# Products of ones in TensorE's order: the feed-forward stages and the router steps of a two-layer kernel

## The reference, cut to what matters

```
x = x + 0.5 * L0_ffn(layernorm(x))      # ffn1
x = x + L0_attn(layernorm(x))
x = x + 0.5 * L0_ffn(layernorm(x))      # ffn2
x = x + 0.5 * L1_ffn(layernorm(x))      # moe1
x = x + L1_attn(layernorm(x))           # retention
x = x + 0.5 * L1_ffn(layernorm(x))      # moe2

def L0_ffn(x):                          # 8 experts of rank 8
    result = x @ base_w.T + base_b
    gating = softmax(x @ router_w.T + router_b)          # then bfloat16
    mid = x @ lora_A
    return result + 2.0 * einsum('bsr,erd,bse->bsd', mid, lora_B, gating)

def L1_ffn(x):                          # 16 experts, 4 of them per token
    scores = sigmoid(x @ router_w.T)
    ... the two best of 4 groups, the four best experts in them, weights tw ...
    routed = sum over the chosen experts of tw * (silu(x @ gate_w) * (x @ up_w)) @ down_w
    return routed + (silu(x @ sh_gate_w) * (x @ sh_up_w)) @ sh_down_w
```

## Time and profile before

| what | us |
|---|---|
| median of 3 runs | 1731.96 |
| lowest and highest of them | 1723.12, 1746.84 |
| the profiled execution, its own time | 1735.6 |
| its span in the trace | 1733.8 |

### The profile page before, as it was taken

The page is one execution under the profiler, slowest core; times in us unless marked ns, Lnnn a source line. Parts: engine busy times, 40 slices in busy tenths (PEclk is TensorE's granted clock), DMA queues, the critical chain, the costliest instruction groups (busy, mean ns, idle before and its releaser), DMA issues. The chain is left out here.

```text
span 1733.8 us, 36975 instructions
## 1 busy us (share of the span) xinstructions
PE 1537.2 (89%) x10054; PEld 1258.9 (73%) x10054; DVE 1167.2 (67%) x4550; ACT 815.3 (47%) x1995; POOL 796.3 (46%) x1129
## 2 busy tenths in 40 slices
PE   6699999999897757999959999999999686699995
PEld 5477777777587546888847888887888574588884
DVE  6448888888575743555548898988898666255554
ACT  2247777777625213444424555555555431244442
POOL 2246666666524240222217786877787504111111
PEclk9759999999956778999979999999999868899998
DMA  4598000000023010001021111111111001000003
GB/s 126 149 300 225 0 0 0 0 0 0 7 80 116 18 37 14 27 26 27 27 72 42 41 38 38 37 37 37 37 37 38 1 2 37 25 26 27 25 27 110
DMA packets 101116, 82.91 MB, mean 48 GB/s; under 512 B 9820, under 2 KB 88351, under 8 KB 100720
## 3 DMA queue, kind: packets, MB, share of 16 engines
q1 hardware_dynamic: 95178, 69.87, 15.1%
q0 software_dynamic: 4416, 9.58, 1.6%
q10 hardware_dynamic: 1382, 1.83, 0.4%
HBM read 23.71 MB, written 40.75 MB: 37 GB/s over the span
## 5 line engine op out<-in xcount | busy, mean ns | idle before, releaser
L892 DVE SCALAR_TENSOR_TENSOR moe_block_act<-banks,moe_taken,moe_block_gated 128x128 f32<-128x128 f32 x592 | 166.8, 344 | 186.4 <-ACT moe_block_gated L936 179.1
L921 POOL DMA_INDIRECT y_rows<-moe_block_y,moe_taken x74 | 71.4, 965 | 383.2 <-ACT moe_block_y L946 383.2
L1181 DVE CUSTOM_DVE_ANT_0 attn_z<-banks,rel_bias 128x128 f32<-128x128 f32 (+1 forms) x512 | 161.9, 353 | 69.9 <-PE banks L1311 63.1
L1229 POOL TENSOR_TENSOR attn_z<-attn_top,attn_z 128x256 f32<-128x256 f32 x256 | 159.3, 630 | 94.2 <-DVE attn_top L1181 93.4
L1706 ACT ACTIVATE ret_normed<-banks,ret_head_shift,ret_head_rstd 128x128 f32<-128x128 f32 x256 | 103.9, 458 | 157.0 <-DVE ret_head_shift L1620 157.0
L936 ACT ACTIVATE moe_block_gated<-banks 128x512 f32<-128x512 f32 x148 | 88.6, 599 | 159.2 <-PE banks L977 159.0
L993 PE MATMUL banks<-moe_down,moe_block_actT 128*128 x1184 | 156.3, 275 | 0.0
L1258 ACT ACTIVATE attn_prob<-banks 128x384 f32<-128x384 f32 x256 | 125.9, 492 | 50.2 <-PE banks L1318 40.2
L1318 PE MATMUL banks<-ident,attn_z 128*128 128x128 f32 x768 | 144.0, 299 | 0.3 <-ACT attn_z L1253 0.3
L993 PEld LDWEIGHTS banks<-moe_down,moe_block_actT 128*128 128x128 f32 x1184 | 143.8, 192 | 0.3
L975 PE MATMUL banks<-moe_hi,moe_block_x_hi 128*128 x296 | 130.8, 442 | 1.6 <-DVE moe_block_x_lo L882 1.5
(11 more groups left out here) (260 smaller groups left out, 4255.4 us busy)
## 6 DMA issues: line engine op xcount, KB each, us to landing
slots<-moe_pad SPq DMA_DIRECT2D x12, 2304.0 KB, 20.0
ret_twins<-ret_twins SPq DMA_DIRECT2D x256, 64.0 KB, 2.0
moe_taken<-slots SPq DMA_DIRECT2D x74, 72.0 KB, 1.8
moe_back<-y_rows SPq DMA_DIRECT2D x16, 256.0 KB, 5.0
moe_stage<-in_moe_w SPq DMA_DIRECT2D x4, 576.0 KB, 7.1
bias_reversed<-scratch SPq DMA_DIRECT2D x1, 2048.0 KB, 9.6
out<-x_res SPq DMA_DIRECT2D x8, 256.0 KB, 4.5
ret_stage<-in_ret_w SPq DMA_DIRECT2D x16, 96.0 KB, 2.2
```

The lines of the kernel that those rows point to most:

```text
L892: last = dve.scalar_tensor_tensor(act_f[:, i, at], ps_u[:, i, at], taken[:, b % RB, column:column + 1], gated[:, i, at], ALU.mult, ALU.mult)
L1181: last = dve.tensor_tensor_reduce(out=z[:, k % Z, cols], in0=ps_s[:, k % 2, cols], in1=bias, scale=1.0, scalar=-3.0e38, op0=ALU.add, op1=A ...
L1229: pool.tensor_tensor(z[:, k % Z, P:WIDTH], top[:, k % Z, 1:2].to_broadcast([P, WIDTH - P]), z[:, k % Z, P:WIDTH], ALU.subtract).then_inc(s ...
```

## The change

A tile `ones` (128 x 512, bfloat16) is filled by GpSimd in the opening block. A helper issues a number of products of it with itself, each 128 x 512, into PSUM. Nobody reads the result, and the helper neither waits nor signals. It is called with 3 products at three places: ahead of the wait of `transpose_x` and of `transpose_om` in both feed-forward stages (into a bank of its own, the eighth), and ahead of the wait of `router` in both routing parts (into `ps_y`, which the shared expert uses only later). This makes 16 calls in each feed-forward stage and 8 in each routing part, 48 calls and 144 products. Nothing is removed.

```diff
+def keep_busy(pe, bank_out, ones, times):
+
+    for _ in range(times):
+        pe.matmul(bank_out, ones[:, 0:P], ones[:, :], start=True, stop=True)
...
         ps_y = bank([P, 2, GT])
+        ps_spare = bank([P, 512])
...
             def transpose_x(it, u):
+                keep_busy(pe, ps_spare, ones, 3)
                 pe.wait_ge(xn_ready, count(it, u))
...
             def transpose_om(it, u):
+                keep_busy(pe, ps_spare, ones, 3)
                 pe.wait_ge(om_ready, count(it, u))
...
             def router(g):
                 s = g * GROUP // SEG
+                keep_busy(pe, ps_y[:, :], ones, 3)
                 pe.wait_ge(x_split, g + 1)
...
+        ones = sb("ones", [P, 512], BF16)
...
                     pool.memset(neg_half[:, :], -0.5)
+                    pool.memset(ones[:, :], 1.0)
```

More of the change, by code:

```diff
@@ L79, in bank_taker, with ffn_lora_phase @@
     return take
-def ffn_lora_phase(nc, tag, banks, used, x_res, ident, neg_half, w, background, x_first=None, x_rest=None, split=None):
+def keep_busy(pe, bank_out, ones, times):
+    for _ in range(times):
+        pe.matmul(bank_out, ones[:, 0:P], ones[:, :], start=True, stop=True)
+def ffn_lora_phase(nc, tag, banks, used, x_res, ident, neg_half, ones, w, background, x_first=None, x_rest=None, split=None):
     U = 4
@@ L316, with moe_phase @@
               "coef": [1, 3, CLASSES - 1], "base": [1, 3, BLOCKS], "region": [P, CLASSES]}
-def moe_phase(nc, tag, banks, used, x_res, ident, neg_half, w, slots, y_rows, background, split=None, finish=None):
+def moe_phase(nc, tag, banks, used, x_res, ident, neg_half, ones, w, slots, y_rows, background, split=None, finish=None):
     with ExitStack() as ctx:
@@ L328, in moe_phase, with moe_route @@
         block_table = sb("block_table", [1, 3, BLOCKS], mybir.dt.int32)
-        moe_route(nc, tag, banks, used, x_res, ident, neg_half, w, slots, block_table, background)
+        moe_route(nc, tag, banks, used, x_res, ident, neg_half, ones, w, slots, block_table, background)
         moe_blocks(nc, tag, banks, used, x_res, ident, w, slots, y_rows, block_table, split, finish)
-def moe_route(nc, tag, banks, used, x_res, ident, neg_half, w, slots, block_table, background):
+def moe_route(nc, tag, banks, used, x_res, ident, neg_half, ones, w, slots, block_table, background):
     I32 = mybir.dt.int32
@@ L1961, in fill_slots @@
                         sync.dma_start(of_blocks[:, lo:hi, :], moe_pad[:, :].unsqueeze(1).to_broadcast([P, hi - lo, ROW])).then_inc(slots_filled[i], 16)
-            ffn_lora_phase(nc, "ffn1", banks, used, x_res, ident, neg_half, lora, load_attention, x_first, x_rest)
+            ffn_lora_phase(nc, "ffn1", banks, used, x_res, ident, neg_half, ones, lora, load_attention, x_first, x_rest)
             flip_bias(nc, banks, used, attn, attn_loaded, bias_spread)
@@ L1994, in split_on_pool @@
                 split_lo(pool, i)
-            ffn_lora_phase(nc, "ffn2", banks, used, x_res, ident, neg_half, lora, load_moe, split=(split_on_scalar, split_on_pool, MOE_PARTS))
+            ffn_lora_phase(nc, "ffn2", banks, used, x_res, ident, neg_half, ones, lora, load_moe, split=(split_on_scalar, split_on_pool, MOE_PARTS))
         retire(nc, used)
@@ L2013, in build @@
                 split_hi, split_lo = weight_split(nc, used, "ret", stage, *ret["projections"], ret_part_loaded, RET_PARTS)
-                moe_phase(nc, "moe1", banks, used, x_res, ident, neg_half, moe | filled(0), d["slots"][0], d["y_rows"], load_retention,
+                moe_phase(nc, "moe1", banks, used, x_res, ident, neg_half, ones, moe | filled(0), d["slots"][0], d["y_rows"], load_retention,
                           split=(split_hi, split_lo, RET_PARTS))
@@ L2026, in store_x @@
             sync.wait_ge(out_stored, GROUPS * 16)
-        moe_phase(nc, "moe2", banks, used, x_res, ident, neg_half, moe | filled(1), d["slots"][1], d["y_rows"], lambda sync: None, finish=store_x)
+        moe_phase(nc, "moe2", banks, used, x_res, ident, neg_half, ones, moe | filled(1), d["slots"][1], d["y_rows"], lambda sync: None, finish=store_x)
 def kernel(**inputs):
```

## The result

The changed kernel takes 1745.3 us in the median of 20 runs, the kernel before 1731.34 us in the median of 20 runs beside them on the same chip: ratio 1.0105, 95% interval 1.0083 to 1.0128. It is slower by about 1%, inside the predicted range, 12 us under the predicted 1757. By the medians the change costs 14.0 us, a ratio of 1.0081. The profiled execution of the changed kernel took 1752.27 us with a span of 1750.4 us, which is 16.6 us more than the span before.

The account below looks back on a forecast made before the run. TensorE at half clock was taken as the bound in ffn2 and both routing parts. ffn1 +7.2, ffn2 -4.9 and routing +10 each gave +22 us on 1735.6, forecast 1757 us, range 1727 to 1777.

Parts of the forecast that it names:

- ffn1 only pays: Rest of ffn1, already at 2.4 GHz before: groups grow from 4.13 to 5.3 us, +7.2 us in all.
- The head at 0±1.5: Stage start to end of ffn1's first projection: 2.6 us of added products offset by 2.5 us from the faster clock.
- I therefore expect the rise at the first step with both transposes: Clock rises ahead of ffn2's first projection and at about 25 us in ffn1, then stays up to the stage's end.
- ffn2 gains 4.9 us: Rest of ffn2 after its head: 39.3 us before, 34.4 us after at the upper clock, -4.9 us.
- The two stages together, +2.3 us: ffn1 and ffn2 summed: +7.2 us in ffn1 and -4.9 us in ffn2.
- Routing parts +10 us each: Clock stays at 1.2 GHz; 8 calls of 1.28 us each, the first hidden by 0.3 us, delay each routing part.
- The sum: Whole kernel: +7.2 - 4.9 + 10 + 10 = +22 us on the profiled 1735.6 us, giving 1757 us.
- Attention's rise moves: width, not a direction: Attention starts some 7 us later; its clock rise may shift either way by luck, up to 12 us.
- the triples lift the routing clock: Rival in the routing parts: -5.5 us instead of +10 in a part; 1742 or 1727 us; chance 0.27.
- the rival's 2.4 us group: Routing group time if the three products lift the clock there, against 3.33 us before; chance 0.27.
- ones do nothing in the feed-forward stages: Rival in ffn1 and ffn2: clock not lifted, groups of 9.6 us, 1787 to 1816 us; chance 0.08.
- My argument from the earlier trace, that a triple alone does not raise the clock: Routing parts: a single triple of 512-column products in moe2 had not lifted the clock, so it stays at 1.2 GHz.

Follow-up runs that it names:

- ffn_only: The changed kernel without the products of ones in the routing parts; 1694.96 us against 1697.29 for the kernel before, ratio 1.0036.
- ffn_zeros: The changed kernel with the tile filled with 0.0 instead of 1.0; 1711.5 us, one execution.
- narrow: The changed kernel with 12 products of 128 columns per call instead of 3 of 512; 1717.54 us, one execution.
- route_only: The changed kernel without the products of ones in the feed-forward stages; 1717.53 us, ratio 1.0153 to the kernel before.
- route_burst: Kernel before plus, in routing parts only, 24 products ahead of the first transpose, 3 ahead of the second, 3 per router step; 1695.16 us against 1697.29, ratio 0.9987.
- route_burst5: Kernel before plus, in routing parts only, 24 products ahead of the first transpose and 5 at each router step; 1684.45 us against 1689.12, ratio 0.9994.
- ffn2_all_burst5: Kernel before plus 3 products ahead of all 16 ffn2 transposes, and in routing parts a burst of 24 and 5 per router step; 1713.33 us against 1728.65, ratio 0.991.
- burst_alone: Kernel before plus only 24 products ahead of the first transpose in both routing parts; 1695.24 us against 1698.52, ratio 0.9991.

## Why the prediction came out right, step by step

**The feed-forward stages over many executions.** One profile says little here, since the rise wanders. Over the profiled executions of all kernels, those with ones at a stage's head only left out:

| stage | without ones | with all triples | change |
|---|---|---|---|
| ffn1 | 42.4 to 48.8, mean 43.9 (8 runs) | 46.7 to 51.4, mean 48.9 (5) | +5.0 us |
| ffn2 | 54.4 to 64.3, mean 57.2 (6) | 52.3 to 56.4, mean 53.1 (6) | -4.1 us |

- *ffn1 only pays: right; its size is +5.0 us on the mean* against +7.2, and the ranges overlap (without ones, one execution with a rise at 44.5 took 48.8). The group is 4.90 us and not 5.3: a triple at the full clock costs about 0.65 us (0.22 us a product, where I took 0.24 from the earlier trace rows), and the rest of the group took 4.90 - 1.30 = 3.60 us where I had 4.13 - 0.24 = 3.89. *The head at 0±1.5: missed in this profile.* The first projection ended 2.1 us later, since the rise came at 33.2 and not at 25. The step that failed is "I therefore expect the rise at the first step with both transposes": it held in `ffn_only`, `ffn_zeros` and `narrow` (26.0, 23.8, 24.3 us), and not in the changed kernel's two executions (33.2, 33.4).
- *ffn2 gains 4.9 us: right*, -7.3 in this profile, -4.1 on the mean. The reason was half seen. Without ones the clock often rises early enough (in `route_only` at 476.5, 20.4 us into its low stretch) and then falls again before the end (497.0). The triples hold it as much as they raise it.
- *The two stages together, +2.3 us*: +0.9 by the table, and `ffn_only`'s ratio of 1.0036 is +6 us with an interval from -1 to +13.
- *Routing parts +10 us each: right.* +9.6 in the profile, 37.5 us in all four executions with three products of 512 columns (two of the changed kernel, `route_only`, `ffn_zeros`), group 4.60 us as forecast, clock 0.50 throughout, the first shared product late by 9.6 us against the first transpose.
- *The sum.* By the means of these runs it is +5.0 - 4.1 + 2 x 9.7 = +20 us, 1.2% of 1731; the two measured ratios are 1.0105 and 1.0135 (+18 and +23 us; by the medians +14 and +25). The predicted 1757 lies 12 us over the median because I put the +22 us on the profiled 1735.6, some 4 us above the median, and because luck that the sum can't hold (attention, moe2's shared part) differs between executions.
- *"Attention's rise moves: width, not a direction"*: shown by the line of 0.42 us above, and by the runs of before, which spread from 1715.9 to 1755.15 us.

**The rivals.** That the triples lift the routing clock is refuted for three products with no burst ahead, but the mechanism exists: behind a burst the rival's 2.4 us group came in `route_burst`, three times, and with two more products at each step the clock held in `route_burst5`. That ones do nothing in the feed-forward stages is refuted by the row of 487.20 to 524.70. My argument from the earlier trace rows, that a triple alone does not raise the clock, was right for the wrong reason where it leaned on width.

**What stays open.** moe2's stretch from the first shared product to the first block was 4.9 us longer in the profile after. That part flips between the two clocks many times, and the windows show a mean clock of 0.76 there against 0.82 before; on a second chip the same stretch took 86.2 us in `route_only`, 85.3 in the changed kernel and 85.1 in `ffn_only`, so the ones ahead of it are not shown to lengthen it. The length goes with the chip: 102 to 107 us where the two kernels were profiled first and 104 on the chip of `ffn2_all_burst5`, 83 to 87 us on the two others. On the longer side VectorE waits at the shared expert's multiply for nothing that the trace names (14.3 us in moe2 of the kernel before, 11.6 in the changed one, none in `route_only`). Its cause is open.

```profile
1419.00:1524.80 105.80, 64.55 (x331) 51.02 (x330) 51.42 (x228) 22.57 (x64) 31.49 (x32) 0.76 0.08 26
```

By the Trainium skill, "TensorE: Matmul & The Clock Gate", Part 1, sustained matmul activity releases the low clock; the row of 539.40 to 560.10 of `burst_alone`, full and at 0.50, does not agree with that taken by itself. By the Trainium skill, "TensorE: Matmul & The Clock Gate", Part 4, transposes don't count as busy in the same way; that is consistent with the fall in that row, but in the routing parts transposes and 16-column products always stand together, and no run parted them.

No run has five products at each router step without the burst, so it is not shown that the routing parts need both.

## What to carry to other kernels

In this kernel filler products paid only where the clock was low for most of a stage in which TensorE was the bound and where they kept it up to the end of it (ffn2, and the routing parts with burst and five); count their price at the low clock for the case in which they don't, since that is the case in which they cost most (here 1.25 us a triple, +9.6 us a routing part). Raising and holding are two amounts, and each is to be measured: here three products at each step neither raised the clock nor held it to the end, while a burst of 24 in the idle time ahead, with five at each step, did, and turned +9.6 us a part into -4.5 us (27.8 to 23.3), for 2.1 us of burst in both. Where the clock's rise is luck, one profile of each kernel compares luck; take lengths by stage over several executions.

## What the runs showed that was not expected

- With products of zeros the clock rose (23.8 and 484.6 us) and stayed up as with products of ones, and so it did with twelve of 128 columns for three of 512, at about the same price (1.24 us). One execution of each.
- A clock once up fell after 4.6 us with no ones, after 8.1 us with three a group, and stayed for 23.2 us with five a group (TensorE records for 3.64 of 4.60, 8.05 of 8.10 and 23.01 of 23.20 us).
- Attention, the same in these kernels, differed by 17 us with the place of its rise (386.4 to 403.8 us).
